# Three buffers for raw weights, casts and bias products at other places, and an earlier fetch of one batch's tokens

## The reference, cut to what matters

```python
# x: 8 batches x 512 tokens x 256 features, all in f32
x = x + 0.5 * ffn(layernorm(x))      # "call 0"
x = x + attn(layernorm(x), weight)   # "global stage": 16 heads over all 512 tokens
x = x + 0.5 * ffn(layernorm(x))      # "call 1", same weights as call 0

# ffn: two layers, each with its own weights
h = shift_token(x)                   # half the features come from the token before
q, k, v = split(h @ wqkv)            # 256 x 1536
q, k = rotary(l2norm(q) * qs), rotary(l2norm(k) * ks)
x = x + local_attention(q, k, v) @ wo        # 8 heads, windows of 128 tokens; wo 512 x 256
h = layernorm(shift_token(x)) * lg + lb
a, g = split(h @ w1 + b1)            # w1 256 x 1364
x = x + (a * gelu(g)) @ w2 + b2      # w2 682 x 256
```

## Time and profile before

| | us |
|---|---|
| median of three runs (lowest, highest) | 3782.51 (3778.07, 3786.26) |
| the profiled execution | 3784.34 |
| its span, first to last instruction | 3782.6 |
| PE busy | 3475.8 (92% of the span) |
| DVE, POOL, ACT busy | 2639.0, 2267.5, 2076.9 |

### The profile page before, as it was taken

The page is one execution under the profiler, slowest core; times in us unless marked ns, Lnnn a source line. Parts: engine busy times, 40 slices in busy tenths (PEclk is TensorE's granted clock), DMA queues, the critical chain, the costliest instruction groups (busy, mean ns, idle before and its releaser), DMA issues.

```text
span 3782.6 us, 72921 instructions
## 1 busy us (share of the span) xinstructions
PE 3475.8 (92%) x21152; PEld 2843.0 (75%) x21152; DVE 2639.0 (70%) x7104; ACT 2076.9 (55%) x4840; POOL 2267.5 (60%) x2307
## 2 busy tenths in 40 slices
PE   4799998999999799999999999995999988899997
PEld 2577777777777588888888888874787777677775
DVE  6677877688888365565555655655877877788884
ACT  2475775567667244444444444443766765667563
POOL 4577666557766355555555555654676766566762
PEclk9899999899999899999999999997999999999998
DMA  4443344434434431222212212104343444334433
GB/s 140 137 151 126 114 142 133 127 111 148 152 115 157 106 73 46 46 52 57 46 45 52 57 46 51 63 17 142 128 152 111 138 136 138 115 122 147 134 110 105
DMA packets 425434, 396.05 MB, mean 105 GB/s; under 512 B 139292, under 2 KB 373416, under 8 KB 425128
## 3 DMA queue, kind: packets, MB, share of 16 engines
q1 hardware_dynamic: 425128, 392.57, 34.5%
HBM read 224.67 MB, written 159.38 MB: 102 GB/s over the span
## 4 chain that ended last, share of the span: by engine, by line
PE 61%; DVE 14%; issue 10%; ACT 7%; POOL 4%; DMA 2%; SPq 1%; DVEq 1%; ACTq 0%; POOLq 0%
PE psum L1446 17%; PE psum L1447 16%; PE psum L1448 16%; PE psum L1582 4%; DVE probs L1152 3%; PE psum L1668 3%; ACT probs L910 3%; PE psum L1554 2%; DVE p_blocks L1174 1%; PE psum L1565 1%; POOL probs L770 1%; ACT L910 1%; DVE turned_qk L1121 1%; DVE nb L1160 1%; POOL ge_lo L809 1%
## 5 line engine op out<-in xcount | busy, mean ns | idle before, releaser
L809 POOL TENSOR_TENSOR ge_lo<-ge,ge_hi 128x512 fp32r<-128x512 f32 x512 | 672.6, 1316 | 528.6 <-PE psum L1448 287.8
L770 POOL TENSOR_SCALAR probs<-probs,rz 128x256 f32<-128x256 f32 (+1 forms) x1024 | 444.0, 453 | 557.6 <-DVE rz L1166 557.6
L983 ACT ACTIVATE ge<-psum 128x512 f32<-128x512 f32 x512 | 306.3, 598 | 669.4 <-PE psum L1668 664.7
L1343 DVE CAST ge_hi<-ge 128x512 fp32r<-128x512 f32 x512 | 266.0, 522 | 505.8 <-ACT ge L983 503.8
L910 ACT ACTIVATE probs<-probs,nb,rq 128x256 f32<-128x256 f32 (+1 forms) x1024 | 574.8, 564 | 51.0 <-DVE nb L1160 49.8
L1152 DVE CUSTOM_DVE_ANT_0 probs<-psum,mask 128x256 f32<-128x256 f32 (+1 forms) x1024 | 336.7, 383 | 96.0 <-issue 47.0
L745 POOL TENSOR_TENSOR rinv<-ssq,minus_half 128x16 f32<-128x16 f32 x124 | 366.2, 2954 | 24.4 <-DVE ssq L1136 17.5
L1446 PE MATMUL psum<-wqkv_hi,hT_hi 128*128 128x512 f32 x768 | 341.7, 445 | 27.0 <-issue 16.8
L1174 DVE STREAM_TRANSPOSE p_blocks<-probs 128x384 f32<-128x384 f32 (+1 forms) x384 | 291.2, 784 | 62.3 <-POOL probs L770 59.6
L1446 PE MATMUL psum<-nT_hi,w_hi 128*128 128x512 f32 x704 | 292.9, 416 | 33.5 <-ACT gate L931 23.9
L1447 PE MATMUL psum<-wqkv_hi,hT_lo 128*128 128x512 f32 x768 | 315.0, 410 | 0.0
(11 more groups left out here) (153 smaller groups left out, 9796.9 us busy)
## 6 DMA issues: line engine op xcount, KB each, us to landing
p_turned<-p_blocks SPq DMA_DIRECT2D x128, 512.0 KB, 2.6
pT<-p_turned SPq DMA_DIRECT2D x512, 128.0 KB, 3.0
p_turned<-p_blocks SPq DMA_DIRECT2D x128, 384.0 KB, 2.6
pT<-p_turned SPq DMA_DIRECT2D x512, 96.0 KB, 2.5
xnext<-stream SPq DMA_DIRECT2D x32, 512.0 KB, 3.9
xmid<-stream SPq DMA_DIRECT2D x32, 512.0 KB, 3.9
gaT<-y_turned SPq DMA_DIRECT2D x256, 64.0 KB, 2.0
y_turned<-probs SPq DMA_DIRECT2D x192, 64.0 KB, 2.9
```

The costliest lines, as they stand in the source:

```text
L770: last = nc.gpsimd.tensor_scalar(pu, pu, rz[:, h, t:t + 1], 1.0, ALU.mult, ALU.mult)
L809: nc.gpsimd.tensor_tensor(ges[1][:, k % 4, :], ge[:, k % 4, :], f32(ges[0][:, k % 4, :]), ALU.subtract).then_inc(S["g_lo"], 1)
L983: nc.scalar.activation(ge[:, k % 4, :], RB[k % 2], ACT.Exp, scale=GSCALE, accum_out=gz[:, h, t:t + 1]).then_inc(S["g_exp"], 1)
```

## The change

The change gives chunk k of the weights one of three slots (k % 3 outside the global stage); the third slot is the memory of `gx`, which only the global stage uses. It moves the fetch of w1's second half to the round's start and of w2 to the place between ld4 and ld5, the six small DMAs to the start of call 0 (layer 0) and into round 1 (layer 1), the casts f0 and f1 ahead of steps in the middle of the drain of the batch before, and the bias products B ahead of A6, into PSUM bank 5 in place of bank 0. The wait for the bias products goes from w2's fetch to the places where a raw w1 is overwritten. The fetch of round 17's tokens goes into the last sequence of the global stage.

```diff
+WB = 3
...
-            "A7 +k3 W2 W3 B +K1 +v0").split()
+            "A6 A7 +k3 W2 W3 +K1 +v0").split()
...
-SP_STEPS = ("+xin wq wo wf0 st0 st1 ld0 ld1 -old st2 st3 ld2 st4 ld3 st5 st6 ld4 wf1 ld5 st7 ld6 ld7 -keep res "
-            "shift wf2").split()
+SP_STEPS = ("+xin wq wo wf0 wf1 st0 st1 ld0 ld1 -old st2 st3 ld2 st4 ld3 st5 st6 ld4 wf2 ld5 st7 ld6 ld7 -keep "
+            "res shift").split()
...
-         "B": (0,)}
+         "B": (5,)}
...
-    gx = [sb(f"gx{r}", [P, NT, D]) for r in range(2)]
+    gx_both = sb("gx", [P, 2, NT, D])
+    gx = [gx_both[:, r] for r in range(2)]
...
+    def slot(k):
+
+        if G_BASE <= k < G_BASE + G_CHUNKS:
+            return (k - G_BASE) % 2
+        return (k - (G_CHUNKS if k >= G_BASE else 0)) % WB
+
+    def before_in_slot(k):
+
+        return [j for j in range(k) if slot(j) == slot(k)]
+
     def w_buf(k):
 
-        return wbuf[k % 2][:]
+        return wbuf[slot(k)][:] if slot(k) < 2 else gx_both[:].rearrange("p s t d -> p (s t d)")[:, 0:3 * INNER]
...
-            if k >= 2:
-                sp.wait_ge(S["w_lo"], k - 1)
+            if before_in_slot(k):
+                sp.wait_ge(S["w_lo"], before_in_slot(k)[-1] + 1)
...
             l, k = stage % LAYERS, w_base(stage)
+            need(sp, S["bias_mm"], min(stage, LAYERS))
             for kt in range(KD):
                 chunk(k + kt, [(w_buf(k + kt), wqkv[l, kt * P:(kt + 1) * P, :])])
...
-            sp.wait_ge(S["bias_mm"], min(stage + 1, LAYERS))
             chunk(k + 2, [(v[:, 0:FJ, :], w2[l, 0:FJ * P, :].rearrange("(k p) d -> p k d", p=P)),
...
             def first(n, call=call):
                 x_ahead(n, None)
+                w_vectors(0)
...
-                        if i == 1 and load < LAYERS:
-                            w_vectors(load)
...
-                    if kind == "xin":
+                    if kind == "xin" and not (isinstance(m, int) and m == ROUNDS + 1):
...
                         p_rows(m, i)
+                        if i == 1 and early is not None and early < LAYERS:
+                            w_vectors(early)
...
                         rows_in(b + 1, 1 - r, 0)
+                    else:
+                        need_apart(sp, (S["g_out"], 16 * (B - 1) + 1))
+                        x_ahead(ROUNDS + 1, None)
```

More of the change, by code:

```diff
@@ L38 @@
 PE_STEPS = ("Q2 v1 v2 S0 K2 Q3 K3 v3 +z0 +z1 S1 -n0 -n1 +k0 +q0 S2 -g0 -a0 -g1 +q1 -a1 S3 S4 -w0 -g2 -g3 S5 S6 "
-            "-a2 -a3 A0 A1 -w1 S7 +k1 -w2 -a4 -g4 A2 A3 -g5 +Q0 +q2 +k2 +Q1 -w3 A4 A5 -w4 -w5 +K0 +q3 W0 W1 A6 "
-            "A7 +k3 W2 W3 B +K1 +v0").split()
+            "-a2 -a3 A0 A1 -w1 S7 +k1 -w2 -a4 -g4 A2 A3 -g5 +Q0 +q2 +k2 +Q1 -w3 A4 A5 -w4 -w5 +K0 +q3 W0 W1 B "
+            "A6 A7 +k3 W2 W3 +K1 +v0").split()
 ACT_STEPS = ("Qc3 Kc3 vh3 +zh0 +zh1 E0 -nh0 -nh1 i0 i1 +sk0 E1 +sq0 -G0 -G1 -u0 E2 -u1 +sq1 E3 i2 -G2 -G3 E4 "
-             "-u2 E5 E6 O0 +sk1 E7 -G4 -u3 O1 -G5 -u4 +Qc0 +Qc1 +sq2 -u5 +sk2 +Kc0 O2 +sq3 O3 f0 f1 +sk3 f2 "
+             "-u2 E5 E6 O0 +sk1 E7 -G4 -u3 O1 -G5 f0 -u4 +Qc0 +Qc1 +sq2 f1 -u5 +sk2 +Kc0 O2 +sq3 O3 +sk3 f2 "
              "+Qc2 +vh0 +vh1 +Kc1 +Kc2 +vh2").split()
 DVE_STEPS = ("X0 -j0 +zl0 -j1 +zl1 X1 R0 -nl0 -nl1 i0 i1 +rk0 X2 R1 V0 +rq0 -y0 +ss0 V1 -y1 X3 R2 X4 i2 +rq1 V2 "
-             "R3 X5 V3 -y2 R4 X6 V4 -y3 R5 X7 P0 R6 V5 V6 +rk1 +ss1 R7 -y4 -y5 P1 V7 +rq2 -F -e +ss2 +rk2 +rq3 "
-             "P2 P3 +ss3 x B f0 +rk3 +Y f1 l r f2").split()
-SP_STEPS = ("+xin wq wo wf0 st0 st1 ld0 ld1 -old st2 st3 ld2 st4 ld3 st5 st6 ld4 wf1 ld5 st7 ld6 ld7 -keep res "
-            "shift wf2").split()
+             "R3 X5 V3 -y2 R4 X6 V4 -y3 R5 X7 P0 R6 V5 V6 +rk1 +ss1 R7 -y4 -y5 f0 P1 V7 +rq2 -F f1 -e +ss2 +rk2 "
+             "+rq3 P2 P3 +ss3 B x +rk3 +Y l r f2").split()
+SP_STEPS = ("+xin wq wo wf0 wf1 st0 st1 ld0 ld1 -old st2 st3 ld2 st4 ld3 st5 st6 ld4 wf2 ld5 st7 ld6 ld7 -keep "
+            "res shift").split()
 POOL_STEPS = ("N0 N1 +b0 -ul0 +p0 -ul1 N2 N3 +b1 +d0 N4 -ul2 N5 N6 -ul3 N7 +c0 -ul4 -ul5 +d1 +p1 +b2 +p2 +c1 +b3 "
@@ L330, in build @@
     names = """apart consts x0_out x0_stats x0_var x0_rs x0_z stage
-        w_in0 w_in1 w_hi w_lo w_small rope_ok bias_mm bias_ok
+        w_in0 w_in1 w_in2 w_vec w_hi w_lo w_small rope_ok bias_mm bias_ok
         x_in xmid_in x_stored shift_in xold_in
@@ L351, in left, with vectors_in @@
         return [t for t in table if load != LAYERS or t not in done]
-    def small_in(stage, last=9):
-        return 16 * (9 * min(stage, LAYERS) + 3 * max(stage - LAYERS, 0) + (last if stage < LAYERS else 3))
+    def vectors_in(stage):
+        return 16 * 6 * min(stage + 1, LAYERS)
     def stage_end(eng, k):
@@ L385, in gw @@
         return gw_[:, c // G_COLS, side, c % G_COLS, :]
+    def slot(k):
[4 more added lines that the diff above has]
+        return [j for j in range(k) if slot(j) == slot(k)]
     def w_buf(k):
-        return wbuf[k % 2][:]
+        return wbuf[slot(k)][:] if slot(k) < 2 else gx_both[:].rearrange("p s t d -> p (s t d)")[:, 0:3 * INNER]
     def g_buf(c):
-        return wbuf[c % 2][:, 0:G_COLS * D]
+        return wbuf[slot(G_BASE + c)][:, 0:G_COLS * D]
     def w_base(stage):
@@ L403, in chunk_in @@
     def chunk_in(eng, k):
-        eng.wait_ge(S[f"w_in{k % 2}"], 16 * sum(CHUNK_DMAS[k % 2:k + 1:2]))
+        eng.wait_ge(S[f"w_in{slot(k)}"], 16 * sum(CHUNK_DMAS[j] for j in before_in_slot(k) + [k]))
     def weights_done(eng, k):
@@ L456, in chunk @@
         def chunk(k, dst_src):
-            if k >= 2:
-                sp.wait_ge(S["w_lo"], k - 1)
+            if before_in_slot(k):
+                sp.wait_ge(S["w_lo"], before_in_slot(k)[-1] + 1)
             for dst, src in dst_src:
-                sp.dma_start(dst, src).then_inc(S[f"w_in{k % 2}"], 16)
+                sp.dma_start(dst, src).then_inc(S[f"w_in{slot(k)}"], 16)
         def w_qkv(stage):
@@ L490, in w_vectors @@
             l = stage % LAYERS
-            sp.dma_start(lnp[l][:, 0, :], ln_g[l].rearrange("(k p) -> p k", p=P)).then_inc(S["w_small"], 16)
-            sp.dma_start(lnp[l][:, 1, :], ln_b[l].rearrange("(k p) -> p k", p=P)).then_inc(S["w_small"], 16)
+            sp.dma_start(lnp[l][:, 0, :], ln_g[l].rearrange("(k p) -> p k", p=P)).then_inc(S["w_vec"], 16)
+            sp.dma_start(lnp[l][:, 1, :], ln_b[l].rearrange("(k p) -> p k", p=P)).then_inc(S["w_vec"], 16)
             b1v = b1t[l][:].rearrange("p (j c) -> p c j", c=2)
@@ L496, in w_vectors @@
                 sp.dma_start(b1v[:, c, 0:FJ], b1[l, lo:lo + FJ * P].rearrange("(j p) -> p j", p=P)
-                             ).then_inc(S["w_small"], 16)
+                             ).then_inc(S["w_vec"], 16)
                 p0 = P // 2 * (1 - c)
                 sp.dma_start(b1v[p0:p0 + HR, c, FJ:FJ + 1], b1[l, lo + FJ * P:lo + HID].rearrange("(p o) -> p o", o=1)
-                             ).then_inc(S["w_small"], 16)
+                             ).then_inc(S["w_vec"], 16)
         def w_2(stage):
@@ L598, in w_g @@
         def w_g(c):
+            if c < KD:
+                sp.wait_ge(S["bias_mm"], LAYERS)
             chunk(G_BASE + c, [(g_buf(c).rearrange("p (k d) -> p k d", d=D),
@@ L853, in w_f @@
             k = w_base(stage) + W_A
-            act.wait_ge(S["w_small"], small_in(stage))
+            act.wait_ge(S["w_vec"], vectors_in(stage))
             if part < KD:
@@ L1039, in w_rope @@
         def w_rope(stage):
-            dve.wait_ge(S["w_small"], small_in(stage, 3))
+            dve.wait_ge(S["w_small"], 16 * 3 * (stage + 1))
             for i in range(2):
@@ L1508, in biases @@
             chunk_in(pe, k + 1)
-            pe.wait_ge(S["w_small"], small_in(stage))
+            pe.wait_ge(S["w_vec"], vectors_in(stage))
             for j in range(FJ + 1):
```

## The result

The changed kernel takes 3757.44 us (median of four runs, 3753.91 to 3761.47), the kernel before 3782.29 beside it: 24.9 us less, ratio 0.9935 with a 95% interval of 0.9918 to 0.9952. The forecast was 3765, with 3748 to 3778 as its range. The profiled execution has a span of 3755.5 us, 27.1 less than before.

A forecast was written before the change was run, and what follows sets the result against it. PE, busy 92% of the span, was taken to set the time. Gains of 8.8 + 6.9 + 0 + 2.0 = 17.7 us from 3784.3, less 1.8 from profile to median, gave 3765 us, range 3748 to 3778.

The forecast's parts named there:

- The border: Between global stage and call 1: PE waits for DVE's subtractions instead of a DMA, gaining 8.8 of 13.72 us.
- Rounds 16 and 24: Ends of these load rounds: time from x to PE's start falls from 12.45 to 9.0 us, gaining 6.9 for both.
- A5's wait: Mid-round wait for pT: 1.5 us gained each in rounds 0 and 8, 0.5 lost each in 16 and 24, net 2.0.
- Rounds 0 and 8: Ends of these load rounds: tail 6.7 us shorter, less 5.0 for B and 1.8 for P2, so nothing gained.
- The wait for P2: Ahead of B at its new place in rounds 0 and 8: another 1.8 us until DVE's P2 empties bank 5.
- The tail from x to PE: End of rounds 0 and 8: from x to PE's resuming, 15.72 us becomes 9.0, 6.7 less.
- The lower bound of this term: Round ends of 0 and 8: -3.6 us each if the wait for P2 doubles.
- The casts: f0 and f1 at their new places on DVE cost nothing, covered by idle time ahead of e; uncovered, 14 to 21 us.
- The loops: DVE's loops of rounds 9 to 14 and 25 to 30 keep their 69.8 and 75.1 us a round.
- The rival's mechanism: Third rival: shifted DVE code makes a loop slow or fast at its returns, 26.5 us either way; chance 0.05 each.
- The clock: Half-clock stretch behind PE's wait at the border: counted as nothing, about 5 us more if the clock stays up.

The follow-up runs named there:

- The run with B late: The changed kernel with the bias products B back behind W3 on PE and their addition last on DVE, in rounds 0 and 8: 3741.6 us.
- the run of the tokens alone: The kernel before with only the fetch of round 17's tokens moved into the global stage's last sequence: 3772.74 us, ratio 0.9978.

## Why the prediction was right, and where it was off

**The border: right.** Forecast 8.8, shown 8.3 in the trace, and alone 8 to 9 in time. That DVE's order would take over from the DMA was the step that mattered: the full wait would have said 15.

**Rounds 16 and 24: the round ends right, the rounds too small.** From x to PE it went from 12.45 to 8.84 in round 24, 3.6 for a forecast of 3.4, and from 12.16 to 7.86 in round 16, 4.3. The two rounds as a whole gave 5.3 and 6.3, 11.6 where the sum had 6.9 less 1.0. In round 24 A5's wait fell from 2.72 to 1.69, where I had booked a loss of 0.5 (in round 16 it rose from 2.65 to 3.38), and the granted clock from the statistics of round 23 to x was 0.98 in place of 0.95.

**Rounds 0 and 8: near in sum by luck, mis-sized in three terms.** B was taken at 5.04 us. It takes 8.2 to 8.3 at its new place, where the granted clock over B is 0.56; a B at 0.98 or 1.00 takes 4.79. The wait for P2 (1.8) was 2.35 and 1.76. Against these stand two errors the other way. The tail from x to PE, taken at 9.0, was 7.90 and 8.07. And A5's wait, for which I took 1.5 each, fell by 4.35 in round 0, from 5.96, which is over the bound of 3.31, and by 2.98 in round 8. The row of round 8 before, and then those of rounds 0 and 8 now:

```profile
726.73 1.98 PE L1582 MATMUL psum<-pT,vs 128*64 128x128 f32 x12 [3.88 <-DMA pT<-p_turned]
```

```profile
125.51 1.09 PE L1600 MATMUL psum<-pT,vs 128*64 128x128 f32 x12 [1.61 <-DMA pT<-p_turned]
...
723.90 1.09 PE L1600 MATMUL psum<-pT,vs 128*64 128x128 f32 x12 [0.90 <-DMA pT<-p_turned]
```

In the other seven kernels with the moved fetches A5 waits 1.3 to 4.4 us in round 0 and up to 2.4 in round 8, so that the fetches shorten the wait is likely, and the size of one trace is chance; which of the moved fetches does it is not shown. The errors nearly cancel in round 0 (0.1 gained where the sum had 1.5). Round 8 gained 4.1, and "in round 8 I take the same" was a reading that the kernel before didn't bear out: B took 6.98 us there and the tail 17.95, not 5.04 and 15.72. The run with B late shows what the sum hid: without B's new place the change would be worth 16 us more. The lower bound of this term is mis-added, too: with the wait for P2 doubled it is 6.7 - 5.0 - 3.6 = -1.9, not -3.6.

**The casts: right in size.** At the old places they cost 15 us more than at the new ones, which is what the prediction had for no cover at all (14 to 21). The cover was named right for two of the four load rounds: ahead of e 10.38 us of idle time went to nothing in round 8 and 8.14 to 0.93 in round 24, so it is used up there. In rounds 0 and 16 there is no e, and what covers the casts was not looked into.

**The loops: the step failed in its form.** "The loops keep their 69.8 and 75.1 us" was wrong for the profiled execution. The slow loop varies between 73.4 and 75.4 a round within one program, so part of the 27.1 us of the trace is luck. The rival's mechanism is real, however, and larger than I gave it credit for: its two terms were 26.5 us in either direction, for five returns of one loop, and 60 idle instructions gain 38.7. The loop of rounds 3 to 6 paid already in the kernel before, which the prediction didn't see: DVE stands 4.08 to 4.53 us for issue at its three returns there, and rounds 4 to 6 take 73.0 to 73.7 us; with 60 memsets they take 69.3 to 69.4. By its place alone the change did not flip a loop. Why a slow round takes 73.4 one time and 75.3 another is open: in the run of the tokens alone the dear ones have a granted clock of 0.98 and the cheap one 1.00, but the changed kernel has a round of 73.30 at 0.98.

**The clock.** I took nothing for it. Over the span the mean granted clock went from 0.968 to 0.972, and at the border from 0.50 to 0.76 in the first 9.5 us:

```profile
2553.60:2563.10 9.50, 7.60 (x26) 5.27 (x26) 4.42 (x15) 2.99 (x9) 0.00 (x0) 0.76 0.56 185
```

At the end of the program it went the other way by 4.8 us. One execution doesn't tell which of it belongs to the change; round 31, at 67.5 us in the changed kernel, takes 64.3 to 66.0 in the other nine. Without the loop of rounds 25 to 30 and the end the trace shows 27.1 - 8.1 + 4.7 = 23.7 us, beside 24.9 in the medians and 17.7 in the sum. The 6 us missing are nearly all in rounds 16 and 24 (11.6 for 5.9); rounds 0 and 8 gave 4.2 for 3.0, the border 8.3 for 8.8, and the others lost 0.4.

## What to carry to other kernels

When a wait goes, look first at the order of the engine that serves the next one: here it set the border (DVE's normalising), and w2's cast, which was ready 0.75 us before x and still came 6.6 us after it. The same work may run at half the clock at another place, as B did behind its wait and A6 and A7 behind B, so a filler is priced by its place, and best put where the time is idle anyway. And where a hardware loop shows a stall for issue at its return, shift its program by some idle instructions before tuning anything else, and look at every loop after it: 60 cured two loops here, 30 cured these and made a third one slow.

## What had not been expected of the hardware

Where a loop body of 275 or 277 DVE instructions lies decides over 3.5 to 6 us a round: 69.1 to 69.9 against 72.9 to 75.8 us with the same work, with a stall of 3.2 to 4.7 us at each return against 0.7. 48 products of one column took 4.79 us at a granted clock of 0.98, 6.98 at 0.65 and 8.27 at 0.56. The last stood behind a wait of 2.35 us, the other two behind none.
